# Small products of a chunked scan, moved from the vector engine's program to GpSimd's

## The chip, the cores and the metric

The kernel runs on one core of one Trainium2 chip. The metric is the device time of one execution in microseconds (us), as the median of several runs. The engines are named as the profile names them: PE (TensorE, matmuls), PEld (its weight loads), DVE (VectorE), ACT (ScalarE), POOL (GpSimd) and SP (SyncE, which here issues the DMAs).

## The reference

The program is a small network over 2048 tokens of 512 features. One attention layer is a gated delta rule with a decay for each of 128 channels in 16 heads. A feed-forward layer, a second attention layer with a chosen set of keys, and a second feed-forward layer follow. Only the recurrence of the first layer is touched:

```python
def step(St, inp):
    kt, qt, vt, at, bt = inp
    Sk = jnp.einsum('bhij,bhj->bhi', St, kt)
    err = Sk - vt
    Sn = at[..., None] * St - (bt[..., None] * err)[..., None] * kt[:, :, None, :]
    ot = jnp.einsum('bhij,bhj->bhi', Sn, qt)
    return (Sn, ot)
...
_, outs = jax.lax.scan(step, S0, (tfirst(k), tfirst(q), tfirst(v), tfirst(a), beta.transpose(1, 0, 2)))
```

`St` is a 128x128 state for each head, `at` the decay, `bt` the weight of the update.

## The kernel before

`program` calls one phase after the other. `scan_phase` (from L956) computes the recurrence. The channel lies on the 128 partitions. It takes the 2048 tokens in 64 chunks of 32 tokens (C), and a chunk in eight blocks of 4 (NBLK). Keys, values, queries and decays come through a ring of 256 tokens (`ring`, in SBUF) which SP fills; eight chunks are one turn of the ring. The first and the last turn are written out, and the six between them are a hardware loop whose body holds eight chunks. Every engine has a program of its own, and semaphores alone order them against each other.

In each chunk b the engines do the following.

- PE multiplies the state `ST` with the chunk's keys and queries into `y_ps` (32 matmuls at L1305) and signals `pq_done`.
- DVE solves the eight blocks one after the other. `solve(b, u, k)` is five instructions, each waiting for the one before: `part` from PSUM (L1610), `res` (L1612), `prod` (L1614), the reduction into `U` (L1617) and `z` into a Z tile (L1620). `decay_y` (L1631) then scales the part of `y_ps` that is still to come, and `decay_z` (L1636) scales older z.
- Between two solves lies a hop. PE transposes z, ACT copies it to `zt`, and PE multiplies it into `y_ps` (L1263 then L1267 in hops 1 and 5, L1255 then L1259 in hops 0, 2, 4 and 6, L1271 then L1276 in hop 3). The next solve waits for that.
- After solve 7 PE transposes `Z32` (L1348), ACT copies it, and PE adds the update to the decayed state (L1355). These matmuls also wait for `st_decayed`, which the four instructions of `decay_state` (L1596) count. ACT then copies the new state to `ST`, and the next chunk begins.

Beside this chain stands work that prepares chunk b+1 or finishes chunk b-1. DVE does these parts of it:

- `stage_keys` (L1519 to L1521): three products of neighbouring keys, after solve 0. PE spreads them to all partitions (`spread_far`, `spread_near`).
- `skip_decay` (L1525): one product into `a12`, after solve 1, read by `far3`.
- `tables` (L1532 to L1540): six products of decays over 2, 4, 8 and 16 tokens (`tot2`, `tot4`, `tot8`, `tot16`) and entries of `before` and `after`, after solve 5.
- the product `V` of `U` and the decays (L1720), after the last `decay_state`. ACT makes `W` of it and PE transposes both.
- `inclusive` (L1601, L1602), `far`, `far3`, `mask23`, `mask4`, `mask_out21`, `mask_out0`, the product into `yo_ps` (L1723), and `invert` (L1558 to L1567) at the end.

POOL's program of this phase is three memsets. The ten instructions listed above for `stage_keys`, `skip_decay` and `tables`, and V, have both inputs in SBUF. In the phase ahead of the scan (`project_phase`), POOL and DVE work at the same time: POOL runs L402, L414 and the folds at L430, DVE the convolution at L390, all with two SBUF inputs. The prediction reads prices from there.

Of the kernel before, what the change touches and what calls it, by code (L numbers as in the profile page):

```python
# [7 lines left out]
ALU = mybir.AluOpType  # L8
# [947 lines left out]
def scan_phase(nc, streams, decays, o_dram, ident, block_masks, pair_mask, T):  # L956
# [6 lines left out]
    with ExitStack() as ctx:  # L963
# [176 lines left out]
        def _(pe):  # L1140
# [72 lines left out]

            def turn_u(c, p):

                pe.wait_ge(v_done, c + 1)
                for g in range(4):
                    t = pe.transpose(w_ps[:, QBC, g, :], U[:, p, 4 * g:4 * g + 4, :].rearrange("p h t -> p (h t)"), idt[:, :])
                t.then_inc(ut_done, 1)
# [280 lines left out]
        @block.gpsimd  # L1500
        def _(pool):
            pool.memset(zlow[:, 1], 0.0).then_inc(init, 1)
            pool.memset(inv[:, :, :, :, :], 0.0).then_inc(init, 1)
            pool.wait_ge(init, NINIT - 1)
            pool.memset(inv[:, :, :, :, 0::5], 1.0).then_inc(init, 1)

        @block.vector
        def _(dve):
            mult, add, sub = ALU.mult, ALU.add, ALU.subtract

            def stage_keys(it, u):

                b = it * BPR + u
                dve.wait_ge(chunk_in[u // BPS], 80 * (it + 1))
                if not (isinstance(b, int) and b < 1):
                    dve.wait_ge(bc_done, 2 * b)
                kb = blocks(KB, u).rearrange("p h b t -> p t h b")
                k = blocks(KK, u).rearrange("p h b t -> p t h b")
                dve.tensor_tensor(stage[:, 0:3], kb[:, 1:4], k[:, 0:3], mult)  # L1519
                dve.tensor_tensor(stage[:, 3], kb[:, 3], k[:, 0], mult)  # L1520
                dve.tensor_tensor(stage[:, 4:6], kb[:, 2:4], k[:, 0:2], mult).then_inc(staged, 1)  # L1521

            def skip_decay(c, u):
                a = blocks(AA, u)
                dve.tensor_tensor(a12[:, :, :], a[:, :, :, 1], a[:, :, :, 2], mult).then_inc(a12_done, 1)  # L1525

            def tables(c, u):
                p = u % 2
                a = at(AA, u)
                a4 = blocks(AA, u)  # L1530
                pairs = tot2[:, p].rearrange("p h (b t) -> p h b t", t=2)
                dve.tensor_tensor(tot2[:, p], a[:, :, 0::2], a[:, :, 1::2], mult).then_inc(tab_step, 1)  # L1532
                dve.wait_ge(tab_step, 6 * c + 1)
                dve.tensor_tensor(tot4[:, p], pairs[:, :, :, 0], pairs[:, :, :, 1], mult).then_inc(tab_step, 1)
                dve.tensor_tensor(before[:, p, :, :, 3], pairs[:, :, :, 0], a4[:, :, :, 2], mult).then_inc(tab_step, 1)
                dve.tensor_tensor(after[:, p, :, :, 0], a4[:, :, :, 1], pairs[:, :, :, 1], mult).then_inc(tab_step, 1)
                dve.wait_ge(tab_step, 6 * c + 2)
                dve.tensor_tensor(tot8[:, p], tot4[:, p, :, 0::2], tot4[:, p, :, 1::2], mult).then_inc(tab_step, 1)
                dve.wait_ge(tab_step, 6 * c + 5)
                dve.tensor_tensor(tot16[:, p], tot8[:, p, :, 0::2], tot8[:, p, :, 1::2], mult).then_inc(tab_step, 1)  # L1540
# [97 lines left out]
            def prologue():  # L1638
                dve.memset(ST[:, :, :, :], 0.0).then_inc(init, 1)
                dve.memset(neg[:, :], -1.0).then_inc(init, 1)  # L1640
                dve.memset(before[:, :, :, :, 0], 1.0).then_inc(init, 1)
                dve.memset(after[:, :, :, :, 3], 1.0).then_inc(init, 1)
                dve.memset(half[:, :, :, :, 0:2], 1.0).then_inc(init, 1)
                dve.wait_ge(init, NINIT)
                dve.wait_ge(const_in, 64)
                stage_keys(0, 0)
                skip_decay(0, 0)
                far(0, 0)
                mask23(0, 0)
                far3(0, 0)  # L1650
                tables(0, 0)
                invert(0, 0)
                mask4(0, 0)

            def body(it, u, left):
# [9 lines left out]
                dve.wait_ge(tab_copied, b + 1)  # L1665
                solve(b, u, 0)
                decay_y(b, u, 0)
                if left:
                    stage_keys(ni, nu)
                decay_z(Z8[:, :, 0:4], Z4[:, :, :], z0 + 1, tot4[:, p, :, 1:2])  # L1670
                solve(b, u, 1)
                decay_y(b, u, 1)
                if left:
                    skip_decay(b + 1, nu)
                solve(b, u, 2)
                decay_y(b, u, 2)
                decay_z(Z16[:, :, 8:12], Z4[:, :, :], z0 + 4, tot4[:, p, :, 3:4])
# [36 lines left out]
                mask_out0(b)  # L1714
                dve.wait_ge(go_masked, 2 * b + 2)
                decay_state(b, 3)
                if not first:
                    dve.wait_ge(w_copied, b)
                    dve.wait_ge(ut_done, 2 * b)
                dve.tensor_tensor(V[:, :, :], U[:, p, :, 0::2], at(AA, u)[:, :, 1::2], mult).then_inc(v_done, 1)  # L1720
                if not first:
                    dve.wait_ge(o_copied, b)
                dve.tensor_tensor(yo_ps[:, :, :], y_ps[:, :, 1, :], half[:, p].rearrange("p h b t -> p h (b t)"), mult).then_inc(yo_step, 1)  # L1723
# [815 lines left out]
```

## Time and profile before

| | us |
|---|---|
| median of 3 runs | 8566.85 |
| lowest, highest run | 8565.0, 8574.71 |
| the profiled execution | 8577.77 |
| its span | 8576.0 |
| the scan's 64 chunks, first solve to last | 1144 to 3834 of the span |
| one chunk | 41.2 to 42.7, and 45.5 to 46.2 at five turns of the loop |
| POOL busy, whole program | 736.0, none of it between 1143 and 3834 |

All times in the rows are from the start of the span. A timeline row gives start, duration, engine, line, operation, output and inputs, shapes, and in brackets how long the engine was idle before it and who ended that. The start of a DVE instruction can lie a little before the end of the one before it, since they overlap. The mean granted clock of PE is a share of the full 2.4 GHz, so 0.5 is 1.2 GHz.

### The profile page before, as it was taken

Reading aid. Unit: us, or ns where it says so; the run is one execution under the profiler, and the core shown is the slowest. Engines: PE = TensorE matmul, PEld = TensorE weight load, DVE = VectorE, ACT = ScalarE, POOL = GpSimd, SP = SyncE. Lnnn points to the kernel's source line nnn. Section 1 sums busy time; section 2 is a strip of 40 time slices with the busy share of each in tenths; the row PEclk is TensorE's granted clock in tenths of the full one; section 3 lists DMA queues with packets and bytes.
Section 4 is the critical chain, followed back from the end, with each engine's and each line's share of the span. In section 5 each row is a group of like instructions: output and inputs, shape, how many; then the busy total and the mean of one; then the engine's idle time right before and its main releaser. Section 6 shows DMA issues by size and latency. Waiting matters only on the chain. (4 is left out here: it accounts for less than half of the span.)

```text
span 8576.0 us, 84049 instructions
## 1 busy us (share of the span) xinstructions
PE 6556.2 (76%) x26502; PEld 4452.5 (52%) x26502; DVE 4972.7 (58%) x8482; ACT 2404.3 (28%) x4766; POOL 736.0 (9%) x360
## 2 busy tenths in 40 slices
PE   2888857777777777767979959645429889998899
PEld 1666645555555555554547844322218722222587
DVE  2888856666666666665663222687887733333322
ACT  1222222222222222224432111344412133333111
POOL 0555500000000000001101101000000000000011
PEclk6999956666666666668989979656655588887899
DMA  4333332322222122212120031111102221111200
GB/s 153 119 137 133 133 90 55 84 55 55 62 77 59 54 62 79 55 34 101 47 71 30 22 113 74 55 30 32 27 18 60 50 45 30 30 39 43 82 26 27
DMA packets 554973, 545.85 MB, mean 64 GB/s; under 512 B 69072, under 2 KB 473296, under 8 KB 529616
## 3 DMA queue, kind: packets, MB, share of 16 engines
q1 hardware_dynamic: 554624, 541.59, 21.4%
q8 instruction: 171, 2.80, 0.1%
q14 instruction: 178, 1.46, 0.1%
HBM read 380.16 MB, written 161.35 MB: 63 GB/s over the span
## 5 line engine op out<-in xcount | busy, mean ns | idle before, releaser
L297 PE MATMUL proj_acc<-proj_xn,proj_w 128*128 128x512 f32 x3072 | 728.4, 400 | 126.3 <-ACT proj_decay L343 91.1
L2313 PE MATMUL attend_ot<-attend_e,attend_v 128*64 128x512 f32 (+3 forms) x1280 | 687.7, 628 | 91.4 <-ACT attend_e L2340 91.4
L297 PEld LDWEIGHTS proj_acc<-proj_xn,proj_w 128*128 128x128 f32 x3072 | 594.0, 194 | 260.8 <-ACT proj_decay L343 94.1
L1937 PE MATMUL csum_sc<-csum_qk 96*128 96x512 f32 (+3 forms) x640 | 289.2, 568 | 395.6 <-ACT csum_e L1961 349.9
L390 DVE SCALAR_TENSOR_TENSOR proj_y<-proj_raw,proj_cw,proj_y 128x2048 f32<-128x2048 f32 x144 | 575.5, 3996 | 19.1 <-DVE proj_y L386 3.0
L1610 DVE TENSOR_TENSOR scan_part<-scan_y_ps,scan_before 128x64 f32<-128x64 f32 x512 | 114.6, 224 | 792.5 <-PE scan_y_ps L1305 494.4
L1370 ACT ACTIVATE scan_zt<-scan_zt_ps 64x128 f32<-64x128 f32 (+2 forms) x448 | 129.1, 288 | 1490.7 <-PE scan_zt_ps L1255 1050.7
L1305 PE MATMUL scan_y_ps<-scan_ring,scan_ST 128*128 128x64 f32 x2048 | 449.8, 420 | 66.3 <-ACT scan_ST L1370 42.8
L1305 PEld LDWEIGHTS scan_y_ps<-scan_ring,scan_ST 128*128 128x128 f32 x2048 | 438.5, 330 | 84.4 <-ACT scan_ST L1370 43.5
L885 POOL TENSOR_TENSOR ffn_hid_low<-ffn_hid,ffn_hid_high 128x512 fp32r<-128x512 f32 x128 | 164.6, 1286 | 3574.5 <-ACT ffn_hid_high L875 3574.5
L938 DVE TENSOR_TENSOR ffn_hid<-ffn_gate,ffn_l 128x512 f32<-128x512 f32 x128 | 88.0, 688 | 582.7 <-PE ffn_l L821 351.8
L2372 DVE SCALAR_TENSOR_TENSOR attend_sc<-attend_far,attend_hcol,attend_sc 128x128 f32<-128x128 f32 x464 | 141.2, 348 | 468.6 <-PE attend_sc L2302 376.8
L1981 DVE TENSOR_REDUCE csum_mx<-csum_sc 128x1 f32<-128x2048 f32 (+15 forms) x256 | 327.5, 1284 | 144.7 <-PE csum_sc L1940 144.7
L1937 PEld LDWEIGHTS csum_sc<-csum_qk 96*128 96x128 f32 x640 | 156.3, 278 | 482.2 <-ACT csum_e L1961 407.8
L2302 PEld LDWEIGHTS attend_sc<-attend_qk 98*128 98x128 f32 x640 | 131.9, 206 | 520.2 <-issue 276.7
L2198 DVE TENSOR_REDUCE cmax_peak<-cmax_sc 128x1664 f32 (+22 forms) x256 | 328.1, 1290 | 116.0 <-PE cmax_sc L2159 113.9
L821 PE MATMUL ffn_g<-ffn_xn,ffn_w 128*128 128x512 f32 x1536 | 372.8, 392 | 10.4 <-issue 10.4
L821 PE MATMUL ffn_l<-ffn_xn,ffn_w 128*128 128x512 f32 x1536 | 369.0, 389 | 0.0
L614 POOL TENSOR_TENSOR mix_sq<-mix_oc 128x512 f32<-128x512 f32 x64 | 66.6, 1040 | 3261.8 <-DVE mix_oc L633 3261.8
L2340 ACT ACTIVATE attend_e<-attend_sc,attend_hcol 128x512 f32<-128x512 f32 (+3 forms) x448 | 271.0, 605 | 251.5 <-PE attend_sc L2302 249.1
L2302 PE MATMUL attend_sc<-attend_qk 98*128 98x512 f32 (+3 forms) x640 | 324.2, 512 | 21.4 <-DMA attend_hcol<-biasT 21.4
L821 PEld LDWEIGHTS ffn_g<-ffn_xn,ffn_w 128*128 128x128 f32 x1536 | 291.0, 190 | 71.7 <-issue 11.2
(260 smaller groups left out, 13467.6 us busy)
## 6 DMA issues: line engine op xcount, KB each, us to landing
scan_abar<-decays SPq DMA_DIRECT2D x256, 256.0 KB, 4.2
csum_qk<-qk SPq DMA_DIRECT2D x96, 256.0 KB
cmax_qk<-qk SPq DMA_DIRECT2D x96, 256.0 KB
attend_qk<-qk SPq DMA_DIRECT2D x96, 256.0 KB
proj_beta_rows<-beta SPq DMA_DIRECT2D x16, 1024.0 KB, 8.1
stream_k<-proj_res SPq DMA_DIRECT2D x16, 1024.0 KB, 3.9
stream_beta_k<-proj_resb SPq DMA_DIRECT2D x16, 1024.0 KB, 3.9
stream_beta_v<-proj_resb SPq DMA_DIRECT2D x16, 1024.0 KB, 3.8
```

Source lines behind the costliest of these rows:

```text
L297: mm = pe.matmul(acc[:, (j * TT + t) % 8, :], w[:, u, wh, j, k, :], xn[:, xh, k, t * TOK:(t + 1) * TOK], start=(p == 0 and k == 0), stop=( ...
L390: dve.scalar_tensor_tensor(y[:, s % 2, :], src, cwt, y[:, s % 2, :], ALU.mult, ALU.add).then_inc(conv_step, 1)
L821: mm = pe.matmul(ps[:, x % 2, :], w[:, u, wh, k, n * P:(n + 1) * P], xn[:, xh, k, t * TOK:(t + 1) * TOK], start=(a == 0 and k == 0), stop= ...
L885: pool.tensor_tensor(hid_low[:, x % 2, :], hid[:, x % 2, :], hid_high[:, x % 2, :].bitcast(F32), ALU.subtract).then_inc(low_done, 1)
L1305: mm = pe.matmul(y_ps[:, h], ST[:, q, g, :], ring[:, 0:2, h, o:o + C], start=(q == 0 and g in (0, 2)), stop=True, skip_group_check=True)
L1937: pe.matmul(sc[:, n % 2, c:c + w], qk[:, u, 0, q * P:(q + 1) * P], qk[:, u, 1, c:c + w], start=True, stop=(c + w < (q + 1) * P))
L1981: dve.tensor_reduce(mx[:, n % 2:n % 2 + 1], sc[:, n % 2, 0:(q + 1) * P], AX.X, ALU.max, negate=True).then_inc(maxed, 1)
L2198: dve.tensor_reduce(peak[:, bass.ds(h * NT + q, 1)], sc[:, n % 2, 0:(q + 1) * P], AX.X, ALU.max, negate=True).then_inc(peaked, 1)
L2302: mm = pe.matmul(sc[:, x % RINGS, lo:TOK], qk[:, u, 1, kt * P:(kt + 1) * P], qk[:, u, 0, g * TOK + lo:(g + 1) * TOK], start=True, stop=not ...
L2313: pe.matmul(ot[:, g % 2, lo:TOK], v[:, u, kt, :], e[:, x % RINGS, lo:TOK], start=(kt == 0), stop=(x == last_of[g])).then_inc(summed, 1)
L2340: op = act.activation(e[:, x % RINGS, near:TOK], sc[:, x % RINGS, near:TOK], ACT.Exp, bias=hcol[:, u, kt:kt + 1], scale=SCALE)
L2372: op = dve.scalar_tensor_tensor(s, fm[:, d - 1, :], hcol[:, u, kt:kt + 1], s, ALU.mult, ALU.add)
```

## The change

The definitions of `stage_keys`, `skip_decay` and `tables`, and the V product, leave DVE's program and stand in POOL's, which becomes a loop over the chunks like the others. Two waits are new, where the order of DVE's own program had kept the buffers apart before: `skip_decay` waits for `inv_step` (the last reader of `a12`) and `tables` for `yo_step` (`inclusive` of two chunks before, the last reader of the tables' other copy). The product V waits for `u_done`, and so does PE's `turn_u`, which waited for `v_done`.

```diff
 def turn_u(c, p):
-    pe.wait_ge(v_done, c + 1)
+    pe.wait_ge(u_done, NBLK * (c + 1))
...
 @block.gpsimd
...
+            def skip_decay(c, u):
+                if not (isinstance(c, int) and c < 1):
+                    pool.wait_ge(inv_step, 8 * c - 6)
+                a = blocks(AA, u)
+                pool.tensor_tensor(a12[:, :, :], a[:, :, :, 1], a[:, :, :, 2], mult).then_inc(a12_done, 1)
+            def tables(c, u):
+                p = u % 2
+                if not (isinstance(c, int) and c < 2):
+                    pool.wait_ge(yo_step, 3 * c - 3)
...
+            def body(it, u, left):
+                b = it * BPR + u
+                first = isinstance(b, int) and b == 0
+                ni, nu = next_of(it, u, 1)
+                if left:
+                    stage_keys(ni, nu)
+                    skip_decay(b + 1, nu)
+                    tables(b + 1, nu)
+                pool.wait_ge(u_done, NBLK * (b + 1))
+                if not first:
+                    pool.wait_ge(w_copied, b)
+                    pool.wait_ge(ut_done, 2 * b)
+                pool.tensor_tensor(V[:, :, :], U[:, u % 2, :, 0::2], at(AA, u)[:, :, 1::2], mult).then_inc(v_done, 1)
...
 @block.vector
...
                 solve(b, u, 0)
                 decay_y(b, u, 0)
-                if left:
-                    stage_keys(ni, nu)
...
-                if left:
-                    skip_decay(b + 1, nu)
...
                 if left:
-                    tables(b + 1, nu)
                     dve.wait_ge(inv_step, 8 * b + 10)
...
-                if not first:
-                    dve.wait_ge(w_copied, b)
-                    dve.wait_ge(ut_done, 2 * b)
-                dve.tensor_tensor(V[:, :, :], U[:, p, :, 0::2], at(AA, u)[:, :, 1::2], mult).then_inc(v_done, 1)
```

First place: DVE's program around hop 5, from solve 5's product to solve 6. Before:

```order
L1614 TENSOR_TENSOR scan_prod<-scan_inv,scan_res 128x256
L1617 TENSOR_REDUCE scan_U<-scan_prod 128x16x4
L1620 TENSOR_TENSOR scan_Z<-scan_U,scan_after 128x16x4
L1631 TENSOR_TENSOR scan_y_ps<-scan_y_ps,scan_tot 128x32x8
L1532 TENSOR_TENSOR scan_tot<-scan_ring 128x256
L1534 TENSOR_TENSOR scan_tot<-scan_tot 128x128
L1535 TENSOR_TENSOR scan_before<-scan_tot,scan_ring 128x128
L1536 TENSOR_TENSOR scan_after<-scan_ring,scan_tot 128x128
L1538 TENSOR_TENSOR scan_tot<-scan_tot 128x64
L1540 TENSOR_TENSOR scan_tot<-scan_tot 128x32
L1596 TENSOR_TENSOR scan_w_ps<-scan_ST,scan_abar 128x512
L1610 TENSOR_TENSOR scan_part<-scan_y_ps,scan_before 128x64
```

And now, on the same engine at the same place:

```order
L1642 TENSOR_TENSOR scan_prod<-scan_inv,scan_res 128x256
L1645 TENSOR_REDUCE scan_U<-scan_prod 128x16x4
L1648 TENSOR_TENSOR scan_Z<-scan_U,scan_after 128x16x4
L1659 TENSOR_TENSOR scan_y_ps<-scan_y_ps,scan_tot 128x32x8
L1624 TENSOR_TENSOR scan_w_ps<-scan_ST,scan_abar 128x512
L1638 TENSOR_TENSOR scan_part<-scan_y_ps,scan_before 128x64
```

The six products of `tables` are gone from between `decay_y` of hop 5 and the first `decay_state`.

Second place: POOL's program, where before there was nothing. One chunk's products of the next chunk, the V product of its own, and the first of the chunk after it:

```order
L1516 TENSOR_TENSOR scan_stage<-scan_ring 128x384
L1517 TENSOR_TENSOR scan_stage<-scan_ring 128x128
L1518 TENSOR_TENSOR scan_stage<-scan_ring 128x256
L1524 TENSOR_TENSOR scan_a<-scan_ring 128x128
L1533 TENSOR_TENSOR scan_tot<-scan_ring 128x256
L1535 TENSOR_TENSOR scan_tot<-scan_tot 128x128
L1536 TENSOR_TENSOR scan_before<-scan_tot,scan_ring 128x128
L1537 TENSOR_TENSOR scan_after<-scan_ring,scan_tot 128x128
L1539 TENSOR_TENSOR scan_tot<-scan_tot 128x64
L1541 TENSOR_TENSOR scan_tot<-scan_tot 128x32
L1560 TENSOR_TENSOR scan_V<-scan_U,scan_ring 128x256
L1516 TENSOR_TENSOR scan_stage<-scan_ring 128x384
```

Eleven instructions stand in a row on POOL, and the `stage` products of the next chunk follow V directly.

## Rows read from the trace of the kernel before

**Rows 1.** Who waited for whom in the scan: total us, times, longest us.

```profile
DVE scan_part L1610 <- PE scan_y_ps L1305: 494.4, 63, 12.0
DVE scan_part L1610 <- PE scan_y_ps L1267: 81.8, 81, 1.4
```

**Rows 2.** Timeline of DVE at solve 5, chunk 28.

```profile
2342.65 0.42 DVE L1602 TENSOR_TENSOR scan_yo_ps<-scan_yo_ps,scan_tot 128x256 f32<-128x256 f32 x1
...
2343.18 0.21 DVE L1636 TENSOR_TENSOR scan_Z<-scan_zlow,scan_tot 128x64 f32<-128x64 f32 x1
...
2343.80 0.23 DVE L1612 TENSOR_TENSOR scan_res<-scan_ring,scan_part 128x64 f32<-128x64 f32 x1
2344.06 0.43 DVE L1614 TENSOR_TENSOR scan_prod<-scan_inv,scan_res 128x256 f32<-128x256 f32 x1
...
2344.97 0.23 DVE L1620 TENSOR_TENSOR scan_Z<-scan_U,scan_after 128x64 f32<-128x64 f32 x1
```

**Rows 3.** The same timeline, DVE from there to solve 6.

```profile
2345.45 0.42 DVE L1532 TENSOR_TENSOR scan_tot<-scan_ring 128x256 f32<-128x256 f32 x1
...
2347.66 0.70 DVE L1596 TENSOR_TENSOR scan_w_ps<-scan_ST,scan_abar 128x512 f32<-128x512 f32 x1 [0.51 <-issue]
2348.27 0.22 DVE L1610 TENSOR_TENSOR scan_part<-scan_y_ps,scan_before 128x64 f32<-128x64 f32 x1
```

**Rows 4.** Timeline of PE at hop 5 of chunk 28.

```profile
2346.03 0.49 PE L1267 MATMUL scan_y_ps<-scan_g,scan_zt 64*128 64x128 f32 x4 [0.44 <-ACT scan_zt L1370]
```

**Rows 5.** Hop 5 of chunk 27: DVE's z, PE, DVE's solve 6.

```profile
2302.68 0.22 DVE L1620 TENSOR_TENSOR scan_Z<-scan_U,scan_after 128x64 f32<-128x64 f32 x1
...
2304.72 0.33 PE L1263 MATMUL scan_zt_ps<-scan_idt,scan_Z 128*128 128x128 f32 x1
2305.50 0.49 PE L1267 MATMUL scan_y_ps<-scan_g,scan_zt 64*128 64x128 f32 x4 [0.44 <-ACT scan_zt L1370]
...
2306.03 0.23 DVE L1610 TENSOR_TENSOR scan_part<-scan_y_ps,scan_before 128x64 f32<-128x64 f32 x1 [0.34 <-PE scan_y_ps L1267]
```

**Rows 6.** Stretches of hop 5, chunks 28, 27: five engines' busy us, clock (seventh), DMA.

```profile
2343.00:2353.00 10.00, 6.21 (x46) 5.22 (x46) 8.93 (x29) 3.28 (x9) 0.00 (x0) 0.98 0.05 12
2299.00:2304.00 5.00, 4.52 (x15) 3.19 (x15) 4.29 (x16) 1.08 (x2) 0.00 (x0) 0.50 0.00 2
```

**Rows 7.** Timeline at hop 0 of chunk 28.

```profile
2327.44 0.69 PE L1259 MATMUL scan_y_ps<-scan_g,scan_zt 32*128 32x64 f32 x4 [0.44 <-ACT scan_zt L1370]
...
2328.30 0.25 DVE L1610 TENSOR_TENSOR scan_part<-scan_y_ps,scan_before 128x64 f32<-128x64 f32 x1
```

**Rows 8.** Timeline at the end of chunk 27 and the start of chunk 28.

```profile
2312.55 0.23 DVE L1620 TENSOR_TENSOR scan_Z<-scan_U,scan_after 128x64 f32<-128x64 f32 x1
...
2313.41 0.70 DVE L1596 TENSOR_TENSOR scan_w_ps<-scan_ST,scan_abar 128x512 f32<-128x512 f32 x1
...
2314.64 2.09 PE L1355 MATMUL scan_w_ps<-scan_ztf,scan_kt 32*128 32x128 f32 x32 [0.69 <-ACT scan_ztf L1370]
...
2324.82 0.23 DVE L1610 TENSOR_TENSOR scan_part<-scan_y_ps,scan_before 128x64 f32<-128x64 f32 x1 [7.56 <-PE scan_y_ps L1305]
```

**Rows 9.** Timeline of the phase ahead, where POOL and DVE overlap.

```profile
339.97 5.57 POOL L414 TENSOR_TENSOR proj_resb<-proj_res,proj_beta_rows 128x2048 f32<-128x2048 f32 x1 [16.48 <-DVE proj_res L371]
...
341.21 6.48 DVE L390 SCALAR_TENSOR_TENSOR proj_y<-proj_raw,proj_cw,proj_y 128x2048 f32<-128x2048 f32 x1 [0.15 <-DVE proj_y L386]
...
373.50 3.14 DVE L390 SCALAR_TENSOR_TENSOR proj_y<-proj_raw,proj_cw,proj_y 128x2048 f32<-128x2048 f32 x1
...
374.57 2.65 POOL L430 TENSOR_TENSOR proj_fold<-proj_fold 128x256 f32<-128x256 f32 x1
```

**Rows 10.** By line and shape: count, busy us, mean ns; and L390's minimum, median, maximum.

```profile
L885 POOL TENSOR_TENSOR ffn_hid_low<-ffn_hid,ffn_hid_high 128x512 fp32r<-128x512 f32 x128 | 164.6, 1286 | 3574.5 <-ACT ffn_hid_high L875 3574.5
L430 POOL TENSOR_TENSOR proj_fold<-proj_fold 128x128 f32<-128x128 f32 x16 | 6.4, 400 | 1.3
...
L390 DVE SCALAR_TENSOR_TENSOR proj_y<-proj_raw,proj_cw,proj_y x144: 2350/3138/6592, 218.4 to 1080.2; 128x2048 f32<-128x2048 f32 x144
```

More of the change, by code:

```diff
@@ L1505, in _, with stage_keys @@
             pool.memset(inv[:, :, :, :, 0::5], 1.0).then_inc(init, 1)
+            mult = ALU.mult
+            def stage_keys(it, u):
+                b = it * BPR + u
+                pool.wait_ge(chunk_in[u // BPS], 80 * (it + 1))
+                if not (isinstance(b, int) and b < 1):
+                    pool.wait_ge(bc_done, 2 * b)
+                kb = blocks(KB, u).rearrange("p h b t -> p t h b")
+                k = blocks(KK, u).rearrange("p h b t -> p t h b")
+                pool.tensor_tensor(stage[:, 0:3], kb[:, 1:4], k[:, 0:3], mult)
+                pool.tensor_tensor(stage[:, 3], kb[:, 3], k[:, 0], mult)
+                pool.tensor_tensor(stage[:, 4:6], kb[:, 2:4], k[:, 0:2], mult).then_inc(staged, 1)
@@ new lines, in skip_decay @@
+            def skip_decay(c, u):
[7 more added lines that the diff above has]
+                    pool.wait_ge(yo_step, 3 * c - 3)
+                a = at(AA, u)
+                a4 = blocks(AA, u)
+                pairs = tot2[:, p].rearrange("p h (b t) -> p h b t", t=2)
+                pool.tensor_tensor(tot2[:, p], a[:, :, 0::2], a[:, :, 1::2], mult).then_inc(tab_step, 1)
+                pool.wait_ge(tab_step, 6 * c + 1)
+                pool.tensor_tensor(tot4[:, p], pairs[:, :, :, 0], pairs[:, :, :, 1], mult).then_inc(tab_step, 1)
+                pool.tensor_tensor(before[:, p, :, :, 3], pairs[:, :, :, 0], a4[:, :, :, 2], mult).then_inc(tab_step, 1)
+                pool.tensor_tensor(after[:, p, :, :, 0], a4[:, :, :, 1], pairs[:, :, :, 1], mult).then_inc(tab_step, 1)
+                pool.wait_ge(tab_step, 6 * c + 2)
+                pool.tensor_tensor(tot8[:, p], tot4[:, p, :, 0::2], tot4[:, p, :, 1::2], mult).then_inc(tab_step, 1)
+                pool.wait_ge(tab_step, 6 * c + 5)
+                pool.tensor_tensor(tot16[:, p], tot8[:, p, :, 0::2], tot8[:, p, :, 1::2], mult).then_inc(tab_step, 1)
@@ new lines, in prologue @@
+            def prologue():
+                stage_keys(0, 0)
+                skip_decay(0, 0)
+                tables(0, 0)
+            def body(it, u, left):
+                b = it * BPR + u
+                first = isinstance(b, int) and b == 0
[9 more added lines that the diff above has]
+                pool.tensor_tensor(V[:, :, :], U[:, u % 2, :, 0::2], at(AA, u)[:, :, 1::2], mult).then_inc(v_done, 1)
@@ L1507, in _, with epilogue @@
+            def epilogue():
+                pass
+            run(pool, prologue, body, epilogue)
         @block.vector
@@ L1509, in _ @@
             mult, add, sub = ALU.mult, ALU.add, ALU.subtract
[L1511 to L1540, printed above, removed]
             def far(c, u):
@@ L1645, in prologue @@
                 dve.wait_ge(const_in, 64)
-                stage_keys(0, 0)
-                skip_decay(0, 0)
                 far(0, 0)
@@ L1650, in prologue @@
                 far3(0, 0)
-                tables(0, 0)
                 invert(0, 0)
```

## The prediction

> **What bounds the kernel now.** The change lies in the scan alone, so I read only the scan, in this order: the list of waits (which engine is late for which), the timeline of one chunk on DVE and PE, and then the same places in the other chunks.
>
> The scan is one serial chain: eight solves on DVE, a hop through PE and ACT after each of seven, and at the chunk's end a long stretch on PE. Idle time of DVE says nothing here; what counts is whether a solve starts when its matmuls end. DVE waits 494.4 us for the state matmuls, once in each chunk [rows 1], for example 7.56 us ahead of 2324.82 [rows 8]. In that stretch DVE has time to spare. It is the place to put work, and nothing taken from DVE there can shorten the chain.
>
> Inside the chunk the question is hop by hop. DVE waited for L1267, which serves hops 1 and 5, 81 times [rows 1]. There are 64 chunks, hence 128 such hops. At hop 1 it waited in all 64, so at hop 5 in only about 17. In the other chunks DVE was late. In chunk 28 PE ended hop 5 at 2346.03 + 0.49 = 2346.52 [rows 4], and solve 6 began at 2348.27 [rows 3], 1.75 us later. In between DVE ran the six products of `tables`, waited 0.51 us and ran a `decay_state` of 0.70 us [rows 3]. This is the place where the change can pay.
>
> **The sum, part by part.** It is made against the profiled execution's span of 8576.0 us and then carried to the median. The profiled execution took 8577.77 us, 10.9 more than the median of 8566.85, so the median after is 8566.85 minus the saving.
>
> *`tables` leave hop 5.* The gap between the end of L1267 and solve 6, taken from the same two rows in every chunk but the last, is 1.23 to 1.75 us in 45 chunks and 0.04 or 0.05 us in 18. The first of the 45 is chunk 0 with 1.23, chunk 28 has the longest, and together they hold 63.2 us. A solve that is waited for starts 0.04 us after its matmul (2305.50 + 0.49 = 2305.99, solve at 2306.03) [rows 5]. Without `tables`, the `decay_state` of 0.70 us would begin at about 2345.5 to 2345.7 and end before 2346.52, so it is covered. Late next is PE. Gain: 63.2 - 45 x 0.04 = 61.4 us. In the 18 chunks nothing is gained: there PE took z only at 2304.72, 1.8 us after DVE had finished it at 2302.68 + 0.22 [rows 5], with a clock of 0.50 against 0.98 at the same hop of chunk 28 [rows 6].
>
> *`stage_keys` leaves hop 0.* PE ended hop 0 at 2327.44 + 0.69 = 2328.13 and solve 1 began at 2328.30 [rows 7]. The slack is 0.17, of which 0.13 can go. Over the 63 gaps I get 8.8 us. So three products that cost 1.6 us on DVE bring 0.14 us a chunk, since hop 0 hid the rest.
>
> *`skip_decay` and V: nothing.* Hop 1 hides the first (DVE waits for L1267 after it anyway), and the 7.56 us ahead of 2324.82 hide the second [rows 8]. If that cover were gone V would cost what a DVE product of 256 elements costs, 0.42 us as in rows 3, in each chunk. `turn_u` stands behind the state matmuls on PE's queue, so its earlier signal changes nothing.
>
> *What POOL takes for the products.* Unhindered rows are 0.40 us for 128 elements and 1.29 for 512 [rows 10], a slope of 2.3 ns an element, so I take 0.70 for 256 and 1.0 for 384. `stage_keys` is then 1.0 + 0.4 + 0.7 = 2.1 us, `skip_decay` 0.4, `tables` 0.7 + 4 x 0.4 + at most 0.4 = 2.5, V 0.7. POOL has 5.8 us of work in a chunk of 42 and was idle. `stage_keys` can begin right after V, at about 2313.5, and its reader `spread_far` comes after hop 1, some 18 us later. `tables` can begin at the end of `inclusive`, 2342.65 + 0.42 = 2343.07 [rows 2], and are needed at the next chunk's start, some 23 us later. POOL's own speed is covered with a wide margin. If that cover were gone, `spread_far` would hold PE in hop 1.
>
> *What POOL does to DVE.* This is the term that costs. L390, a DVE instruction with two SBUF inputs, takes 2.35 us at the least and 6.59 at the most [rows 10]. The one that started at 341.21 ended at 347.69. POOL's L414 had run to 339.97 + 5.57 = 345.54, and 345.54 + 2.15 is 347.69 [rows 9]. So DVE stood until POOL's whole instruction was over. It holds the other way: POOL's fold of 256 elements started at 374.57, DVE's instruction ended at 373.50 + 3.14 = 376.64, and POOL's ended at 377.22, only 0.58 later [rows 9]. The 2.65 us of that row is waiting, not work. The two take turns. Whoever waits when the other ends goes next.
>
> The Trainium skill says the same in "SBUF — State Buffer", section "SBUF: two separate sides": VectorE instructions with two SBUF inputs and GpSimd's share one pair of ports as an exclusive lock, held for the whole instruction. By that page, 5.8 us of POOL's work a chunk could all stand in DVE's way; rows 9 agree with it for two large instructions.
>
> Where do they meet? `res`, `prod`, `z` and `decay_z` have two SBUF inputs; `part`, `decay_y` and the masks have one in PSUM, and I take them as free of it. `tables` start at about 2343.15, just when solve 5 runs. Step by step, by rows 2: `tot2` on POOL meets `decay_z` (2343.18). If DVE is first, `tot2` ends near 2343.97 and `res`, due at 2343.80, slips by 0.1. `tot4` then runs 0.3 and `prod` slips by 0.25. One of the next two products meets `z`, which slips by 0.1 to 0.3. That is 0.45 us. If POOL is first, `decay_z` waits for all of `tot2` and the sum is 0.6 to 0.9. At the least nothing but `z` is met, 0.2; at the most every one of the four waits for a full product, 0.5 + 3 x 0.3, about 1.2 with gaps between. I take 0.45, because DVE follows a signal of its own in 0.03 to 0.04 us and POOL has a wait with an address to work out first. Only the 45 chunks pay: in the 18 others PE is 1.8 us late itself. Cost: 45 x 0.45 = 20.3 us (9 to 54).
>
> The second meeting is at the chunk's end. V waits for three signals, so it starts some 0.25 us after U and lasts to about 2313.5. The last `decay_state`, which also has two SBUF inputs, is due at 2313.41 and goes next, ending near 2314.15. PE needs it at 2314.64 [rows 8]. I take this as free, with an upper bound below. `stage_keys` and `skip_decay` then meet `invert`, which slips by up to 2.5 us into the 7.56 us of idle time.
>
> The Trainium skill, in "GPSIMD Engine Reference", section "Performance pitfalls for Q7 kernels", says reads with a stride over 8 bytes cost half as much again. The `stage` products and two of `tables` read with a stride of 16 bytes. By it the cost at hop 5 would be an estimated 10 us higher, and no row of this trace shows such a stride alone.
>
> *The clock.* PE is at full clock for some 10 us of each chunk. In chunk 28 that includes hop 5 and in chunk 27 it does not [rows 6]. The 18 cold chunks last 42.6 us against 41.8 for the warm ones in the loop. In the written-out turns, where a chunk takes 41.2, fourteen of the fifteen with a successor are warm. With 41.8 - 1.34 - 0.14 + 0.45 = 40.8 us for a warm chunk, some of the 18 should turn warm, each worth 42.5 - 40.8 = 1.7 us. Between 0 and 30 us, I take half, 15.
>
> Sum: 61.4 + 8.8 - 20.3 + 15 = 65 us saved. Span 8576 - 65 = 8511, **median 8566.85 - 65 = 8502 us**.
>
> **The rivals.**
>
> *The lock eats the gain.* POOL wins each meeting at hop 5, the cost is 1.2 us in 45 chunks (54 us), and the clock does not help: 61.4 + 8.8 - 54 = 16, so 8551 us. For it: the products of `tables` stand back to back, and all of them are up in just the two us of solve 5. Against it: DVE's instructions need POOL's absence only four times, and rows 9 show turns, not a queue.
>
> *Slower: the state update waits behind `stage_keys`.* On POOL the `stage` products follow V without a signal between. If V ends before 2313.41, the first of them (384 elements, 1.0 us, perhaps 1.45) gets its turn and `decay_state` is late. It would run to 2315.0 or 2315.5 in place of 2314.11, and PE's update waits: 0.35 to 0.85 us in each of 63 chunks, warm and cold, 22 to 54 us. With a cost at hop 5 of 0.9 us (40), this gives 70.2 - 40 - 54 = -24, or 8591 us. The point from which it decides: V must be over in 0.83 us from the start of z at 2312.55. If V starts 0.1 us after U, it is; if its three waits take 0.25 us, it is not. The change as a whole loses once the two meetings cost over 70.2 / 63 = 1.11 us a chunk together.
>
> *More than forecast.* The meetings cost 0.2 us and nearly all cold chunks turn warm: 61.4 + 8.8 - 9 + 30 = 91, so 8476 us.
>
> *The change doesn't move the work.* The order of DVE's program shows all eleven products gone and POOL's shows them, so I give this nothing.
>
> **How the numbers follow.** Chances: forecast 0.55 (8480 to 8535), more than forecast 0.07, the lock eats the gain 0.18, slower 0.20. The range has to reach into both of the last, so 8472 to 8590; the likeliest case's own range is 8480 to 8535. A measurement of this kernel can tell about 0.2% from no change, here 17 us. Under 8549.7 lie the first two cases; the third, at 8551, lies mostly within. Faster 0.62, same 0.17, slower 0.21.
>
> **What would show it.** (1) The gap at hop 5: DVE's wait for L1267 should count near 128, not 81, with a `part` starting 0.04 us after PE. (2) At solve 5 `prod` or `res` should last longer than their 0.43 and 0.23 us; the excess over 63 chunks is the cost of the lock. (3) The last `decay_state` should still start about 0.86 us after z; if it lasts over 1.4 us, or L1355 has a wait on DVE, the slower rival is at work. (4) POOL should be busy some 6 to 9 us a chunk, waiting included. (5) The clock at hop 5: more chunks with it near 1.0. The forecast falls if `spread_far` waits for POOL, if DVE's instructions with one PSUM input lengthen too, or if the clock's pattern turns against hop 5.

## The result, and the profile after

The changed kernel took 8513.2 us (median of 4 runs, 8506.69 to 8519.21) against 8565.92 (8562.54 to 8574.71) for the kernel before on the same chip. The ratio is 0.9937, 95% interval 0.992 to 0.9954. That is 52.7 us or 0.6% less, with the whole interval below 1, and 11 us short of the forecast.

The profiled execution took 8506.69 us, with a span of 8504.9 and a mean granted clock of 0.752 (0.745 before). The first solve starts at 1145.9 us of the span and the last at 3774.8. This stretch, from the start of the first solve to the start of the last, is called the scan below. It lasts 2628.9 us; before it was 2689.3. So the profiles show 60.4 us less in the scan. The part behind it is the same code in every kernel here, and took between 4721 and 4750 us in the eleven profiles. Spans therefore carry some 30 us of noise that has nothing to do with the change, and I read causes from the scan alone.

These lines of the list of waits (who waited for whom in the scan: us in total, times, longest) answer [rows 1]:

```profile
POOL scan_tot L1533 <- DVE scan_yo_ps L1630: 1535.8, 62, 28.7
POOL scan_V L1560 <- DVE scan_U L1645: 550.2, 64, 40.1
DVE scan_part L1638 <- PE scan_y_ps L1305: 368.2, 63, 9.7
DVE scan_part L1638 <- PE scan_y_ps L1259: 169.7, 130, 1.4
DVE scan_part L1638 <- PE scan_y_ps L1267: 126.3, 128, 2.0
```

Solve 6 now waits for L1267 in all 64 chunks: 128 times in place of 81. DVE still waits for the state matmuls 63 times, for 368.2 us in place of 494.4, mostly because the six instructions of `invert` at the chunk's end take 4.9 us where they took 2.6. POOL is idle for four fifths of the scan. It has 1284.0 us of busy time in the whole program, 548 more than before, or 8.7 a chunk, waiting included.

Here is DVE at solve 5 and hop 5 of chunk 26, the place of [rows 2] and [rows 3]:

```profile
2237.95 0.42 DVE L1630 TENSOR_TENSOR scan_yo_ps<-scan_yo_ps,scan_tot 128x256 f32<-128x256 f32 x1
2238.29 0.28 DVE L1581 TENSOR_TENSOR scan_lag<-scan_w_ps,scan_a 128x128 f32<-128x128 f32 x1
2238.48 0.67 DVE L1664 TENSOR_TENSOR scan_Z<-scan_zlow,scan_tot 128x64 f32<-128x64 f32 x1
2239.07 0.21 DVE L1638 TENSOR_TENSOR scan_part<-scan_y_ps,scan_before 128x64 f32<-128x64 f32 x1
2239.32 0.31 DVE L1640 TENSOR_TENSOR scan_res<-scan_ring,scan_part 128x64 f32<-128x64 f32 x1
2239.66 0.70 DVE L1642 TENSOR_TENSOR scan_prod<-scan_inv,scan_res 128x256 f32<-128x256 f32 x1
...
2240.85 0.28 DVE L1648 TENSOR_TENSOR scan_Z<-scan_U,scan_after 128x64 f32<-128x64 f32 x1
...
2241.39 0.68 DVE L1624 TENSOR_TENSOR scan_w_ps<-scan_ST,scan_abar 128x512 f32<-128x512 f32 x1
2242.49 0.22 DVE L1638 TENSOR_TENSOR scan_part<-scan_y_ps,scan_before 128x64 f32<-128x64 f32 x1 [0.42 <-PE scan_y_ps L1267]
```

And POOL in the same stretch, then PE:

```profile
2238.46 0.61 POOL L1533 TENSOR_TENSOR scan_tot<-scan_ring 128x256 f32<-128x256 f32 x1 [24.57 <-DVE scan_yo_ps L1630]
2239.15 0.40 POOL L1535 TENSOR_TENSOR scan_tot<-scan_tot 128x128 f32<-128x128 f32 x1
2239.51 0.58 POOL L1536 TENSOR_TENSOR scan_before<-scan_tot,scan_ring 128x128 f32<-128x128 f32 x1
2240.04 0.76 POOL L1537 TENSOR_TENSOR scan_after<-scan_ring,scan_tot 128x128 f32<-128x128 f32 x1
```

```profile
2238.33 0.44 PE L1259 MATMUL scan_y_ps<-scan_g,scan_zt 32*128 32x64 f32 x4 [0.44 <-ACT scan_zt L1370]
...
2241.96 0.49 PE L1267 MATMUL scan_y_ps<-scan_g,scan_zt 64*128 64x128 f32 x4 [0.44 <-ACT scan_zt L1370]
```

PE ends hop 5 at 2241.96 + 0.49 = 2242.45 and solve 6 starts at 2242.49, 0.04 later. Of the 1.75 in [rows 3, 4] nothing is left. But PE had ended hop 4 at 2238.33 + 0.44 = 2238.77, and solve 5 started only at 2239.07, 0.30 later. It waited for `decay_z` (L1664), which took 0.67 us where it takes 0.21 alone [rows 2]. `decay_z` asked at 2238.48, and POOL's `tot2` had started at 2238.46 and ran to 2239.07. Then `res` took 0.31 for 0.23, `prod` 0.70 for 0.43 and z 0.28 for 0.23.

At the chunk's end (the place of [rows 8]), DVE, then POOL, then PE:

```profile
2249.02 0.22 DVE L1648 TENSOR_TENSOR scan_Z<-scan_U,scan_after 128x64 f32<-128x64 f32 x1
...
2249.88 0.70 DVE L1624 TENSOR_TENSOR scan_w_ps<-scan_ST,scan_abar 128x512 f32<-128x512 f32 x1
2250.49 0.69 DVE L1739 TENSOR_TENSOR scan_yo_ps<-scan_y_ps,scan_half 128x512 f32<-128x512 f32 x1
2251.09 1.42 DVE L1586 TENSOR_TENSOR scan_mid<-scan_inv 128x256 f32<-128x256 f32 x1
```

```profile
2249.06 0.89 POOL L1560 TENSOR_TENSOR scan_V<-scan_U,scan_ring 128x256 f32<-128x256 f32 x1 [7.70 <-DVE scan_U L1645]
2249.92 2.14 POOL L1516 TENSOR_TENSOR scan_stage<-scan_ring 128x384 f32<-128x384 f32 x1
2252.02 1.02 POOL L1517 TENSOR_TENSOR scan_stage<-scan_ring 128x128 f32<-128x128 f32 x1
```

```profile
2251.10 2.09 PE L1355 MATMUL scan_w_ps<-scan_ztf,scan_kt 32*128 32x128 f32 x32 [0.69 <-ACT scan_ztf L1370]
```

The last `decay_state` starts 0.86 us after z and takes its usual 0.70, and PE's update waits for ACT alone. V ended at 2249.06 + 0.89 = 2249.95 and `decay_state` had asked at 2249.88, so DVE got the next turn by 0.07 us. In all 64 chunks this margin lay between 0.07 and 0.12 us. POOL's first `stage` product stood until 2250.58, and 1.48 of its 2.14 us lie behind that.

Over all chunks (the gaps between PE's last matmul and the solve that waits for it): the gap at hop 5 summed to 63.9 us before and to 2.7 after. The gap at hop 0 fell from 0.18 to 0.04. The gap ahead of solve 5 rose from 0.04 to 0.30. The mean chunk went from 42.26 to 41.29 us. From solve to solve, summed over the 63 chunks that have a successor, the way from solve 5 to 6 shortened by 60.3 us and that from solve 0 to 1 by 8.8, and the way from solve 4 to 5 grew by 9.3. No other way from solve to solve changed by more than 1.0.

### The profile page after: what moved, and what is told of

Read it like the earlier page. It is cut to its first block and busy times, and to the rows that moved or that the text cites. A ratio compares the mean times of both kernels' runs of the same rounds, so it can differ in the third digit from the quotient of the medians.

```text
span 8504.9 us, 84170 instructions
## 1 busy us (share of the span) xinstructions
PE 6511.4 (77%) x26502; PEld 4423.8 (52%) x26502; DVE 4935.3 (58%) x7778; ACT 2405.3 (28%) x4766; POOL 1284.0 (15%) x1064
## 5 line engine op out<-in xcount | busy, mean ns | idle before, releaser
L390 DVE SCALAR_TENSOR_TENSOR proj_y<-proj_raw,proj_cw,proj_y 128x2048 f32<-128x2048 f32 x144 | 575.5, 3997 | 19.1 <-DVE proj_y L386 2.4
L1638 DVE TENSOR_TENSOR scan_part<-scan_y_ps,scan_before 128x64 f32<-128x64 f32 x512 | 113.7, 222 | 781.9 <-PE scan_y_ps L1305 368.2
L2377 DVE RECIPROCAL attend_inv<-attend_ot 32x512 f32<-32x512 f32 x64 | 214.3, 3349 | 183.3 <-PE attend_ot L2329 182.9
```

The costliest lines, as they stand in the source:

```text
L390: dve.scalar_tensor_tensor(y[:, s % 2, :], src, cwt, y[:, s % 2, :], ALU.mult, ALU.add).then_inc(conv_step, 1)
L2377: dve.reciprocal(inv[:, g % 2, :], ot[DH:2 * DH, g % 2, :]).then_inc(inverted, 1)
```

## The experiments

Nine more kernels were run. In the table "warm" is the median time of a chunk in the loop in which PE reaches hop 5 in time (the five long chunks at the turns of the loop are left out), and "cold" the number of chunks, of 63, in which PE is late there because its clock is still low (solve 6 comes over 4.0 us after solve 5 and follows PE by 0.05 or less). Scan, warm and cold come from one profiled execution of each kernel. The ratio is to the kernel before on the same chip, since its median varied between 8566 and 8587 from chip to chip.

| kernel | median us | ratio (95%) | scan us | warm chunk | cold |
|---|---|---|---|---|---|
| before | 8565.92 | 1 | 2689.3 | 41.90 | 18 |
| the changed kernel | 8513.2 | 0.9937 (0.992 to 0.9954) | 2628.9 | 41.01 | 5 |
| tables_on_dve | 8559.06 | 0.9985 (0.9972 to 0.9998) | 2679.0 | 41.71 | 16 |
| tables_at_chunk_end | 8494.76 | 0.9924 (0.99 to 0.9949) | 2612.7 | 40.49 | 15 |
| v_in_halves | 8596.1 | 1.0029 (1.0016 to 1.0043) | 2706.6 | 41.92 | 23 |
| padded | 8596.09 | 1.0032 (1.0016 to 1.0048) | 2716.5 | 42.01 | 26 |
| decay_z_first | 8501.34 | 0.9914 (0.9897 to 0.993) | 2620.9 | 40.89 | 3 |
| end_padded | 8488.59 | 0.9903 (0.9887 to 0.992) | 2616.9 | 40.91 | 2 |
| end_mask4 | 8470.58 | 0.9877 (0.9861 to 0.9894) | 2592.0 | 39.61 | 28 |
| mask4_pad512 | 8485.98 | 0.9887 (0.9858 to 0.9915) | 2611.5 | 40.16 | 23 |
| mask4_pad1152 | 8496.92 | 0.9899 (0.9862 to 0.9936) | 2616.4 | 40.93 | 2 |

### Which of the moved products bring the time

One part undone: `tables` stand in DVE's program again, after solve 5 as before; the rest stays on POOL.

```diff
 @block.vector
...
                 decay_y(b, u, 5)
                 if left:
+                    tables(b + 1, nu)
                     dve.wait_ge(inv_step, 8 * b + 10)
```

> The changed kernel with the six products of tables back on DVE after solve 5; the key products, a12 and V stay on POOL. Theory (only what stands between the end of a hop's matmuls and the next solve counts): the hop 5 gap of 1.2 to 1.75 us comes back in some 45 chunks, the 0.13 us at hop 0 stays gained, so the scan from first to last solve takes 2689.3 - 8.8 = 2680 us, against 2628.9 in the changed kernel, and the median is about 8557. Rival (the saving goes with the work taken off DVE): 2.65 of the 4.54 us a chunk stay moved, so 58% of the 52.7 us are kept, about 8535, scan near 2654.

The scan took 2679.0 us, as expected (2680), and not the 2654 of the rival. The five products that left the other places bring 10.3 us of the 60.4, of which 8.8 lie between solve 0 and solve 1. The remaining 50.1 come with `tables`. The gap at hop 5 is back, over 0.5 us in 47 chunks.

### What the turns at solve 5 cost

`tables` stay on POOL but start at the end of the chunk, when z of solve 7 is done and DVE is about to wait for the state. For that `tot2` needs four copies instead of two.

```diff
-        tot2 = sb("tot2", [P, 2, H, 2 * NBLK])
+        tot2 = sb("tot2", [P, 4, H, 2 * NBLK])
...
             def tables(c, u):
...
-                    pool.wait_ge(yo_step, 3 * c - 3)
+                    pool.wait_ge(z_done, Z_PER * (c - 1))
```

> The changed kernel, but tot2 has four copies instead of two and POOL's tables wait only for the last z of two chunks before, so that they follow the key products and a12 at the end of the chunk, where DVE waits for the state matmuls. Theory (the exclusive turns between POOL and DVE cost 0.67 us at solve 5 in each warm chunk): 58 x 0.67 = 39 us go, scan 2590, median about 8474, prod of solve 5 back at 0.43 us and decay_z at 0.21. POOL then has about 6.5 us of work in DVE's 7 us of idle time; if it overruns, solve 0's products are met instead and up to 0.3 us a chunk is given back. Rival (the longer solve 5 has another cause than POOL's tables): scan stays near 2629, median 8513.

The timeline of DVE at solve 5, chunk 25, and PE at hop 4:

```profile
2190.34 0.22 DVE L1664 TENSOR_TENSOR scan_Z<-scan_zlow,scan_tot 128x64 f32<-128x64 f32 x1
2190.80 0.23 DVE L1638 TENSOR_TENSOR scan_part<-scan_y_ps,scan_before 128x64 f32<-128x64 f32 x1 [0.25 <-PE scan_y_ps L1259]
2191.06 0.23 DVE L1640 TENSOR_TENSOR scan_res<-scan_ring,scan_part 128x64 f32<-128x64 f32 x1
2191.32 0.42 DVE L1642 TENSOR_TENSOR scan_prod<-scan_inv,scan_res 128x256 f32<-128x256 f32 x1
```

```profile
2190.32 0.44 PE L1259 MATMUL scan_y_ps<-scan_g,scan_zt 32*128 32x64 f32 x4 [0.44 <-ACT scan_zt L1370]
```

Every one of DVE's products has its own duration back, and solve 5 follows PE by 0.04. A warm chunk fell from 41.01 to 40.49 us. So the turns at solve 5 cost 0.52 us in each warm chunk. By the rows of one chunk I get 0.26 + 0.40 = 0.66; they differ in part because PE ends hop 4 between 2.91 and 3.06 us after solve 4 in warm chunks, the later the later its clock rises, and its median is 0.08 later here. The cause of the cost is shown: the same products by the same engine, in another place, cost nothing.

The scan still missed its expectation by 23 us (2612.7 for 2590): a warm chunk regained 0.52 us for the 0.67 expected, and not all stayed warm. The 58 warm chunks had become 48. This made the clock the open question.

### Whether the order of the first two requests matters

The one `decay_z` that lost its turn by 27 ns is moved ahead of `inclusive`:

```diff
                 decay_y(b, u, 4)
+                decay_z(Z8[:, :, 0:4], Z4[:, :, :], z0 + 8, tot4[:, p, :, 5:6])
                 if not first:
                     inclusive(b - 1, pu)
                 if left:
                     far3(b + 1, nu)
-                decay_z(Z8[:, :, 0:4], Z4[:, :, :], z0 + 8, tot4[:, p, :, 5:6])
```

> The changed kernel with one instruction moved: the last product of decay_state(b, 5), the one into Z, is asked for ahead of the part of solve 5, so that VectorE's request stands before GpSimd's tot2 and not 27 ns behind it. Lock theory (the turn at solve 5 is lost because GpSimd came first): solve 5 starts some 0.04 us behind TensorE again instead of 0.30, of which later turns may give back 0.1; over 58 warm chunks 9 to 15 us, scan 2614 to 2620 us instead of 2629, median 8498 to 8504. Rival (the order of the two requests doesn't matter, GpSimd's products cost the same wherever they fall): scan 2629, median 8513.

(In this expectation the function is called `decay_state`; it is `decay_z`.) DVE and POOL at solve 5, chunk 26:

```profile
2230.52 0.22 DVE L1638 TENSOR_TENSOR scan_part<-scan_y_ps,scan_before 128x64 f32<-128x64 f32 x1 [0.23 <-PE scan_y_ps L1259]
...
2231.03 0.52 DVE L1642 TENSOR_TENSOR scan_prod<-scan_inv,scan_res 128x256 f32<-128x256 f32 x1
...
2232.04 0.57 DVE L1648 TENSOR_TENSOR scan_Z<-scan_U,scan_after 128x64 f32<-128x64 f32 x1
```

```profile
2231.96 0.57 POOL L1537 TENSOR_TENSOR scan_after<-scan_ring,scan_tot 128x128 f32<-128x128 f32 x1
```

Solve 5 is on time again, but POOL's products stand back to back, and z now lost 0.34 us to L1537. The gain is 0.12 us in a warm chunk (40.89 for 41.01) and 8.0 us in the scan, two cold chunks fewer included. The rival of no effect falls, and the size I expected, 9 to 15 us, was too large. This kernel still pays 0.40 us a warm chunk against the version with the tables at the end (40.89 against 40.49).

### The rival at the chunk's end, provoked

V in two halves, the second of them behind the `stage` products, so that V's first part ends early.

```diff
+            def v_rest(u):
+                pool.tensor_tensor(V[:, 8:16, :], U[:, u % 2, 8:16, 0::2], at(AA, u)[:, 8:16, 1::2], mult).then_inc(v_done, 1)
...
-                pool.tensor_tensor(V[:, :, :], U[:, u % 2, :, 0::2], at(AA, u)[:, :, 1::2], mult).then_inc(v_done, 1)
+                pool.tensor_tensor(V[:, 0:8, :], U[:, u % 2, 0:8, 0::2], at(AA, u)[:, 0:8, 1::2], mult)
```

> The changed kernel with V on POOL cut into two products of 8 heads each: the first where V was, the second after the next chunk's key products. The first ends about 0.35 us earlier, before DVE asks for its last decay_state. Theory (whoever waits when the other ends goes next, and V now ends only 0.08 us after DVE asks): the first key product, 1.48 us, gets its turn, decay_state ends about 1.3 us later, PE's state update starts 0.6 to 0.8 us later in every chunk: scan 2629 + 63 x 0.7 = 2673, median 8557. Rival (DVE goes ahead of POOL whenever both want it, or decay_state doesn't meet POOL at all): no change, scan 2629.

POOL, DVE and PE at the end of chunk 25, and a line of the list of waits:

```profile
2236.67 0.56 POOL L1566 TENSOR_TENSOR scan_V<-scan_U,scan_ring 128x128 f32<-128x128 f32 x1 [7.69 <-DVE scan_U L1651]
2237.19 1.63 POOL L1516 TENSOR_TENSOR scan_stage<-scan_ring 128x384 f32<-128x384 f32 x1
```

```profile
2237.49 1.88 DVE L1630 TENSOR_TENSOR scan_w_ps<-scan_ST,scan_abar 128x512 f32<-128x512 f32 x1
```

```profile
2239.61 1.67 PE L1355 MATMUL scan_w_ps<-scan_ztf,scan_kt 32*128 32x128 f32 x24 [1.59 <-DVE scan_w_ps L1630]
```

```profile
PE scan_w_ps L1355 <- DVE scan_w_ps L1630: 99.8, 62, 2.1
```

V's half ended at 2237.23, the `stage` product took the next turn, and `decay_state`, which asked at 2237.49, stood until 2238.82. It lasted 1.88 us, and PE's update waited for it in 62 chunks. The stretch from solve 7 to the next solve 0 grew from 13.68 to 14.59 us in the median chunk, and by 50 us over all of them, as it grew less in the written-out turns and at the turns of the loop. The scan took 2706.6 us, 77.7 more than the changed kernel and 34 more than expected; the other 27 us lie between solves 4 and 6 and came with cold chunks, 23 for 5. The kernel is slower than the one before. The rival at the chunk's end was real, "no change" falls, and the changed kernel stays clear of it by 0.07 us.

### What sets the number of cold chunks

First, work that nothing reads is put into the chain of the changed kernel, a memset of 128x1024 on DVE between its wait for the state matmuls and solve 0:

```diff
                 dve.wait_ge(tab_copied, b + 1)
+                dve.memset(pad[:, :], 0.0)
                 solve(b, u, 0)
```

> The changed kernel with one more DVE instruction in each chunk, a memset of 128x1024 ahead of solve 0, that touches nothing else. It adds some 0.8 to 0.9 us to the path of each of the 64 chunks, 54 us, so a warm chunk takes 41.9 us as in the kernel before. Theory (which chunks have full clock at hop 5 hangs on the chunk's period; before, at 41.8 us, 18 of 63 were cold, in the changed kernel, at 41.0, 5): cold chunks go back to 15 to 18, another 1.56 x 12 = 19 us: scan 2629 + 54 + 19 = 2702, median 8586. Rival (the share of cold chunks has another cause): 5 cold chunks, scan 2683, median 8567.

A chunk grew by some 1.0 us, more than expected, cold chunks went from 5 to 26 (15 to 18 were expected), and the scan took 2716.5 us (2702 expected). That could still be the ill effect of any disturbance. The opposite case is the same edit with half the memset in the version with tables at the chunk's end, whose chunks are shorter:

> The version with the tables at the chunk's end, plus a memset of 128x512 on VectorE ahead of solve 0 that nothing reads (about 0.62 us a chunk, 39 us over the scan), so that a warm chunk takes some 41.0 us as in the changed kernel and not 40.4. Theory (which chunks have TensorE cold in the solves is set by the loop's period, and 41.0 us is a good one): cold chunks 15 to about 5, and some 20 of the 39 us come back, scan about 2630 us. Rival (the cold chunks come from where the tables stand, not from the period): 15 cold chunks again, scan 2652 us.

Here the added work took the cold chunks from 15 to 2. The memset lengthens the stretch from solve 7 to solve 0 by 0.5 us a chunk, 31 us in all, and the scan grew by 4.2 us, to 2616.9 (2630 expected). Of the 31 us, 22 came back between solves 4 and 6, and 4 between solve 0 and 1, where `part` takes 0.16 us behind the memset in place of 0.22. The rival's 2652 is out.

Then a version that shortens the chunk in earnest. In the version with tables at the end, DVE waits 0.42 us ahead of solve 6, while hop 7 ends on DVE's own work (solve 7 starts 1.73 us behind PE). One mask product moves from the one to the other:

```diff
                 decay_state(b, 0)
+                if left:
+                    mask4(b + 1, np_)
                 solve(b, u, 6)
...
                 if left:
-                    mask4(b + 1, np_)
                     dve.wait_ge(gch_masked, 2 * b + 4)
```

> The version with the tables at the chunk's end, with the first product of the next chunk's masks (0.68 us on VectorE) moved from behind solve 6 to ahead of it, where VectorE waits 0.42 us for TensorE. Theory (hop 7 waits for VectorE's own work, hop 6 for TensorE): the product costs 0.26 us ahead of solve 6 and saves 0.68 behind it, 0.42 us a chunk, 26 us over the scan, scan about 2586 us and median about 8468, if the number of cold chunks stays at 15; each cold chunk more or less is worth some 1.8 us. Rival (hop 7 waits for TensorE or GpSimd instead): the 0.26 us are lost, scan 2629.

Solve 6 now starts 0.13 us behind PE and solve 7 1.08 behind it; a warm chunk fell from 40.49 to 39.61. That is more than the 0.42 forecast, since hop 5's end cost only 0.09 us instead of 0.26 and the chunk's end gained some. But 28 chunks are cold. The scan took 2592.0 us, 20.7 less and 6 more than expected. Its median of 8470.58 and ratio of 0.9877 are the best here, and the interval lies below that of the changed kernel. Its profiled execution, at 8490.35, was 19 us slower than the next of its four, so the 28 need not be its usual count.

The granted clock of PE in a warm chunk and in a cold one of this kernel, in the five us from 19 us after solve 0 (busy us of five engines, clock, DMA):

```profile
2177.00:2182.00 5.00, 4.56 (x38) 4.16 (x36) 4.76 (x16) 1.88 (x7) 0.00 (x0) 1.00 0.00 2
2216.60:2221.60 5.00, 4.56 (x19) 3.73 (x20) 3.23 (x9) 1.33 (x6) 0.00 (x0) 0.63 0.00 0
```

PE is busy for the same 4.56 us in both. With a clock of 1.00 it ran 38 matmuls in it, with 0.63 it ran 19. In the cold chunk most of the stretch passed at the lower level of 1.2 GHz: with the two levels 1 and 0.5, a mean of 0.63 is three quarters of it.

Last, dead work of two sizes, memsets of 128x512 and 128x1152, in this fastest kernel, to see whether its 28 cold chunks belong to its order of work or to its length:

> The version with the tables at the chunk's end and the mask product moved, plus a memset of 128x512 on VectorE ahead of solve 0 that nothing reads (0.5 us a chunk net, as measured, 32 us over the scan): a warm chunk would take about 40.2 us. Theory (the loop's period sets which chunks are cold): cold chunks fall from 28 to between 12 and 22, scan 2592 + 32 - (6 to 16) x 1.9 = 2594 to 2612 us. Rival (this kernel's own order makes 28 cold chunks, whatever the period): scan 2624 us.

> The same with a memset of 128x1152 (about 1.15 us a chunk net, 72 us over the scan): a warm chunk would take about 40.85 us, the period at which the kernel with tables at the end and a smaller memset had 2 cold chunks of 63. Theory (period): at most 6 cold chunks, scan 2592 + 72 - 22 x 1.9 = 2622 us at most, so that 72 us of work that nothing reads cost 30 or less. Rival (the order of the kernel): 28 cold chunks, scan 2664 us.

At 40.16 us a warm chunk there were 23 cold ones (one more than expected, scan 2611.5, at the upper end). At 40.93 there were 2, and the scan took 2616.4 instead of 2592 + 72 = 2664. The kernel's order is not the cause.

Sorted by the length of a warm chunk, the eleven profiles read: 39.61 us with 28 cold, 40.16 with 23, 40.49 with 15, 40.89 with 3, 40.91 with 2, 40.93 with 2, 41.01 with 5, 41.71 with 16, 41.90 with 18, 41.92 with 23, 42.01 with 26. Kernels of nearly the same length have nearly the same count, whatever was done to reach it, and the count has its low point just under 41 us. Each count is that of one execution, and executions of one kernel differ, those of v_in_halves by 40 us, so a difference of a few chunks means little. The mean granted clock, on record for every execution, bears out the large one: it was 0.750 to 0.753 in all 14 executions of the four kernels with 5 cold chunks or fewer, and 0.750 at most in all executions of the others.

The clock records of the eleven traces show how the length does this. In each loop chunk the granted clock rises from 0.5 to 1 once. It does so 16.2 to 18.3 us after solve 0 in all warm chunks, ahead of solve 5, and 21.6 to 23.2 us after it in all cold ones. From chunk to chunk this moment moves against solve 0. In the kernel before it comes earlier from one warm chunk to the next and then late: 17.5, 16.6, 22.6 in chunks 25 to 27. In tables_at_chunk_end it comes later each time, until the chunk is cold: 17.2, 17.5, 18.0, 21.9 in chunks 23 to 26. In the changed kernel, whose warm chunk of 41.01 us lies between those two lengths, it hardly moves: 16.8, 16.8, 16.7, 16.7 in chunks 24 to 27. Why the rise comes when it does was not found out.

## Why the prediction was right, and where it was off

The median came out at 8513.2 for 8502 forecast, inside the likeliest case's own range of 8480 to 8535. By its steps:

- **`tables` leave hop 5**, 61.4 us. Measured 63.9 - 2.7 = 61.2. PE was next, and the `decay_state` of 0.70 us is covered, as argued.
- **`stage_keys` leaves hop 0**, 8.8 us. Measured (0.18 - 0.04) x 63 = 8.8, and 10.3 for all the parts other than `tables` together, by tables_on_dve.
- **The turns at solve 5**, 20.3 us. This term was mis-sized: it measured 23 to 30 us for the 45 chunks (0.52 to 0.66 each), and 30 to 38 over the 58 warm ones. The step that failed was which engine asks first. I took DVE to be first because POOL has an address to work out. My own two times, 2343.15 for `tot2` and 2343.18 for `decay_z`, already had POOL ahead, and I set them aside. `far3`'s L1581, 0.28 us on DVE, stands between `inclusive`, whose end releases POOL, and `decay_z`, so DVE's quick answer to its own signals did not help. POOL came 27 ns ahead. The branch I had priced at 0.6 to 0.9 was the one that came true, at 0.52 to 0.66. The branch I took, at 0.45, measured 0.40 once decay_z_first had made it true. `prod`, `res` and z did wait as said.
- **The clock**, 15 us. Thirteen of the 18 cold chunks turned warm, each worth 42.6 - 41.0 = 1.6 us: 21 us. The direction was argued from one comparison of lengths and held, by luck: the expected 40.8 us lay next to the low point of the count. That a chunk only 0.3 us shorter has 15 cold ones again was not seen.
- **V and `decay_state`**, nothing. It was nothing, but not for the reason given. V started 0.08 us after U and not 0.25; it was late enough only because it too had to wait, for z, so that it lasted 0.89 us instead of 0.71. The rival's point was V's end 0.83 us after the start of z; it came 0.93 after.
- **POOL's prices.** 256 elements took 0.61 (0.70 forecast), 128 took 0.40 (0.40). The `stage` product of 384 was too cheap in the sum at 1.0: ahead of the scan, where DVE does nothing, it took 1.64. L1524, which reads with the same stride of 16 bytes, took the forecast 0.40:

```profile
1133.14 1.64 POOL L1516 TENSOR_TENSOR scan_stage<-scan_ring 128x384 f32<-128x384 f32 x1 [17.28 <-DMA scan_ring<-stream_beta_v]
...
1136.48 0.40 POOL L1524 TENSOR_TENSOR scan_a<-scan_ring 128x128 f32<-128x128 f32 x1
```

L1517, which has as many elements as L1524 and the same stride, took 0.67, so the stride alone does not set the price. The rule in the Trainium skill's "GPSIMD Engine Reference", section "Performance pitfalls for Q7 kernels", that such strides cost half as much again, would by estimate make 1.5 of the 1.0 and 0.6 of the 0.40. The trace agrees with neither number. The error cost nothing here, since `stage_keys` runs in idle time.
- **POOL and DVE take turns**, from large instructions in another phase [rows 9]. The chunk rows show it for instructions of 0.2 us as well, and `part` and `decay_y`, with one input in PSUM, kept 0.21 to 0.23 and 0.42 us beside POOL's products. That the one engine stands for the other's whole instruction is what "SBUF — State Buffer", section "SBUF: two separate sides", of the Trainium skill says, and the rows agree: `decay_z` took 0.67 us for 0.21.

With the measured terms the sum is 61.2 + 8.8 - (23 to 30) + 21 = 61 to 68 us, against 60.4 in the scan. (The 13 newly warm chunks pay for the turns too, which is already in their 1.6 us.) The forecast of 65 was thus near because two errors, turns too cheap by 3 to 10 us and the clock's gain too small by 6, nearly cancelled. The signs came out as named: 128 waits for L1267, `prod` and `res` longer, `decay_state` 0.86 us after z, POOL at 8.7 us a chunk, more warm chunks.

Of the rivals, "the lock eats the gain" had the right winner at the first meeting and the wrong price, as only part of POOL's products fell on DVE's. "Slower" had the right mechanism and missed its point by 0.1 us, as v_in_halves showed.

## What to carry to other kernels

When small products move from DVE to POOL, look less at how long POOL takes than at what DVE does with two SBUF inputs in just those microseconds, and let a signal start POOL's work where DVE waits for someone else: the same products cost 0.52 us a chunk beside a solve and nothing at the chunk's end. Where one of POOL's instructions follows another without a signal, work out who asks first to the last 0.1 us, or add the order by hand, because 0.07 us stood between this gain of 0.6% and the loss of 0.3% in v_in_halves. In a loop whose TensorE clock changes inside each turn, count the turns with a high and a low clock before and after an edit, since 31 us of added work moved the scan by only 4.

## What the runs showed of the hardware that was not expected

- Dead work can be almost free: 0.5 us a chunk cost 4.2 us in 63 chunks, mostly because 13 chunks regained the full clock ahead of solves 5 and 6. With some 1.2 us a chunk (77 us) the scan grew by 24.4.
- Shortening has falling returns for the same reason. From a warm chunk of 40.91 us to one of 39.61, 1.3 x 63 = 82 us, the scan gained 24.9.
- Under such turns the profile's durations of POOL include waiting. L1516 shows 2.14 us behind `decay_state` and 1.64 where DVE is idle; L1537 shows 0.76 beside a solve and 0.57 at the chunk's end (tables_at_chunk_end).
- Lost time moves along. When `decay_z` was given its turn, the z of the same solve lost 0.34 us, so that the 0.26 us regained ahead of solve 5 brought 0.12 in the chunk.
